# Group weights loaded from ScalarE's queue, rows first on SyncE's, and the router's masks turned between two output blocks

## What is computed

```python
x = x + tanh(g_xattn[0]) * xattn0(layernorm(x), ctx, Wq, w_kc_q, w_kc_kv, W_qr, W_kr, Wo)
x = x + tanh(g_ffn[0])   * moe0(layernorm(x), Wr, br, W1, b1, W2, b2, A1, B1, A2, B2)
x = x + tanh(g_xattn[1]) * xattn1(layernorm(x), ctx, Wq, Wkv_expand, Wout)
x = x + tanh(g_ffn[1])   * ffn1(layernorm(x), U, V, W1, b1, W2, b2)

# xattn0: 16 heads, latent attention with rotated keys
q_big = einsum('bshk,hkq->bshq', (h @ Wq.T), w_kc_q);  q_r = einsum('bshq,hqr->bhsr', q_big, W_qr)
kv = kv_c * cos + rotate_half(kv_c) * sin;             k_r = einsum('bld,hdr->bhlr', kv, W_kr)
ctx_c = einsum('bhsl,bld->bhsd', softmax(q_r k_r), kv)
out = einsum('bhsd,hkd->bshk', ctx_c, w_kc_kv).reshape(b, s, H * K) @ Wo.T
# moe0: top 2 of 8 experts; each adds a rank-16 update (A1, B1) to a shared hidden layer of 2048
```

## Time and profile before

| what | us |
|---|---|
| median of three runs | 1389.22 (1384.52 to 1389.39) |
| the profiled execution, its own time | 1386.96 |
| its span in the trace | 1385.0 |
| TensorE busy in the span | 1354.4 (98%) |
| VectorE busy | 920.6 (66%) |
| ScalarE busy | 517.3 (37%) |
| GpSimd busy | 418.3 (30%) |
| DMA queue of SyncE, share of 16 engines | 29.2% |

### The profile page before, as it was taken

How to read it: one execution, slowest core, us unless ns; L and a number is a source line. 1 busy time by engine, 2 the same in 40 slices (tenths; PEclk the granted TensorE clock), 3 DMA queues, 4 the chain that set the end, 5 groups by cost and what they waited for, 6 DMA issues and landing times.

```text
span 1385.0 us, 20435 instructions
## 1 busy us (share of the span) xinstructions
PE 1354.4 (98%) x7644; PEld 1097.6 (79%) x7644; DVE 920.6 (66%) x1775; ACT 517.3 (37%) x1569; POOL 418.3 (30%) x463
## 2 busy tenths in 40 slices
PE   7899999999999999999999999999999999999999
PEld 5688888888788788878887888788876788878887
DVE  5566566665674777786678667776988777734443
ACT  2444454444464322231113111311137777712221
POOL 3122423222254443201111112114428865530000
PEclk9899999999999999999999999999999999999999
DMA  7643444333454232210121112112334131131111
GB/s 265 183 143 112 145 145 129 123 113 124 134 156 119 80 94 73 82 56 17 45 88 31 50 39 84 43 46 74 101 110 134 43 104 64 60 118 50 54 46 46
DMA packets 98246, 128.90 MB, mean 93 GB/s; under 512 B 11724, under 2 KB 58956, under 8 KB 98148
## 3 DMA queue, kind: packets, MB, share of 16 engines
q1 hardware_dynamic: 98148, 127.60, 29.2%
HBM read 90.86 MB, written 36.70 MB: 92 GB/s over the span
## 4 chain that ended last, share of the span: by engine, by line
PE 85%; DVE 7%; DMA 3%; ACT 2%; issue 1%; SPq 1%; POOL 1%; DVEq 0%; ACTq 0%
PE bank L118 81%; PE bank L121 4%; DMA PYZ<-pscr 2%; SPq L170 1%; DMA pscr<-PYZ 1%; DVE PYZ L164 1%; ACT Pb L124 1%; DVE XR L140 1%; DVE XR L137 1%; DVE AH L130 0%; DVE STG L130 0%; ACT PT L124 0%; DVE st L152 0%; DMA XR<-in_x_dram 0%; DVE sm L146 0%
## 5 line engine op out<-in xcount | busy, mean ns | idle before, releaser
L118 PE MATMUL bank<-XT,AR 128*128 128x512 f32 x1152 | 280.3, 393 | 0.3 <-DVE AR L130 0.2
L118 PE MATMUL bank<-AR 128*128 128x512 f32 x1056 | 262.3, 397 | 6.0 <-DVE Msb L127 5.0
L118 PEld LDWEIGHTS bank<-XT,AR 128*128 128x128 f32 x1152 | 213.8, 188 | 48.6 <-issue 1.5
L118 PEld LDWEIGHTS bank<-AR 128*128 128x128 f32 x1056 | 193.7, 188 | 52.4 <-DVE Msb L127 5.4
L124 ACT ACTIVATE STG<-bank,b1c 128x512 f32<-128x512 f32 x128 | 88.3, 690 | 388.9 <-PE bank L118 321.1
L118 PE MATMUL bank<-AR,CT 128*128 128x512 f32 x768 | 194.3, 397 | 1.7 <-DVE CT L130 1.7
L118 PE MATMUL bank<-AR,AH 128*128 128x512 f32 x768 | 185.9, 390 | 0.0
L118 PEld LDWEIGHTS bank<-AR,AH 128*128 128x128 f32 x768 | 143.6, 188 | 30.7 <-issue 1.1
L127 DVE CAST AH<-STG 128x512 fp32r<-128x512 f32 x192 | 92.7, 483 | 112.1 <-PE bank L118 96.9
L118 PEld LDWEIGHTS bank<-AR,CT 128*128 128x128 f32 x768 | 141.2, 190 | 30.4 <-DVE CT L130 2.6
L127 POOL CAST BA<-STG 128x256 fp32r<-128x256 f32 x64 | 31.0, 485 | 400.0 <-PE bank L118 251.8
(11 more groups left out here) (138 smaller groups left out, 1872.0 us busy)
## 6 DMA issues: line engine op xcount, KB each, us to landing
pscr<-PYZ SPq DMA_DIRECT2D x30, 512.0 KB, 2.9
PYZ<-pscr SPq DMA_DIRECT2D x120, 128.0 KB, 3.0
XR<-scr SPq DMA_DIRECT2D x52, 256.0 KB, 2.8
XR<-in_x_dram SPq DMA_DIRECT2D x32, 256.0 KB, 4.1
scr<-XR SPq DMA_DIRECT2D x32, 256.0 KB, 2.2
STG<-in_Wq_dram SPq DMA_DIRECT2D x8, 512.0 KB, 5.3
STG<-in_WoT_dram SPq DMA_DIRECT2D x8, 512.0 KB, 6.6
STG<-in_W1L_dram SPq DMA_DIRECT2D x16, 256.0 KB, 2.7
```

The lines of the kernel that those rows point to most:

```text
L118: return self.e.matmul(o, w, x, start=start, stop=stop, skip_group_check=True) if self.e else Nothing()
```

## The change

- The weight loads of the groups leave SyncE. A new `prep_load(p)` issues all five from ScalarE: groups 0 and 1 at the start of its program, each later group right after ScalarE's evictions of the group whose buffer it takes (`prep_b(old)`).
- On SyncE x tile 0 comes first, then ident, x tiles 1 to 3, ctx, cs, WkrT, and then g4 and the two bf16 constants, which have a semaphore of their own (`d_ib`); their readers, in the third phase, now wait for it.
- In round 33 the transposes of the masks stand between `wo1(31, (0,))` and `wo1(31, (1,))`.
- On VectorE, `final1` of blocks 2 and 3 stands behind the CT remainders and the row turn (u = 11, 19, 27), and at the end behind `masks_b`. In `router_b` the three instructions on w12c and w1c stand behind the mask values; `tail_x` waits for them.

```diff
+        d_ib = sig("d_ib", 16)
...
-            pe.wait_ge(*d_id[2])
             prep_a(0)
+            pe.wait_ge(*d_id[0])
...
-                    wo1(31, (0, 1))
+                    wo1(31, (0,))
+                    mask_turn(0, 7)
+                    wo1(31, (1,))
...
+            def prep_load(p):
+                g, old = stg_of(p), stg_before.get(p)
+                if old is not None:
+                    ac.wait_ge(*ps.full(("M", old)))
+                    ac.wait_ge(*ps.full(("G", old, 1)))
+                    ac.wait_ge(*ps.full(("A", old)))
+                ac.dma(sKq[g], i["kcqT"][p]).then_inc(*d_Kq[g].mark(p))
+                ac.dma(sWr[g], i["Wqr"][p]).then_inc(*d_Wr[g].mark(p))
+                ac.dma(sKc[g], i["kckv"][p]).then_inc(*d_Kc[g].mark(p))
+                ac.dma(sWo[g], i["WoT"][p]).then_inc(*d_Wo[g].mark(p))
+                ac.dma(sWq[g], i["Wq0"][p]).then_inc(*d_Wq[g].mark(p))
+
             def prep_b(p):
                 for h in range(2):
                     ac.wait_ge(*ps.full(("G", p, h)))
                     hi_of(("G", p, h), GG[p][h][0], ps.ap(("G", p, h))[:, :])
                 ac.wait_ge(*ps.full(("A", p)))
                 hi_of(("A", p), GA[p][0], ps.ap(("A", p))[:, :])
+                for n, old in stg_before.items():
+                    if old == p:
+                        prep_load(n)
...
+            prep_load(0)
+            prep_load(1)
             ac.wait_ge(*d_g[0])
             ac.act(tg[:, :], g4[:, :], ACT.Tanh).then_inc(*c_tg.mark(0))
...
-                if 4 <= u < NU and (u - 4) % 8 == 7:
-                    final1((u - 4) // 8, 2)
-                    final1((u - 4) // 8, 3)
-                if u == 34:
-                    final1(3, 2)
-                    final1(3, 3)
...
                 if u < NU and 3 <= p <= 6:
                     ln_turn(*after1(m), p - 3)
+                if 4 <= u < NU and (u - 4) % 8 == 7:
+                    final1((u - 4) // 8, 2)
+                    final1((u - 4) // 8, 3)
...
                     masks_b(0)
+                    final1(3, 2)
+                    final1(3, 3)
```

More of the change, by code:

```diff
@@ L850, in tensor @@
                     stA0(0)
-                    wo1(31, (0, 1))
+                    wo1(31, (0,))
+                    mask_turn(0, 7)
+                    wo1(31, (1,))
                 if u == 34:
                     wo1(31, (2, 3))
-                if u == 33:
-                    mask_turn(0, 7)
                 if u == 32:
@@ L946, in scores3 @@
                 ks = [ps.take(("s3", u, j), 4 + j) for j in range(4)]
+                pe.wait_ge(*d_ib[1])
                 for j in range(4):
@@ L1384, in seed3 @@
             def seed3(u, j):
+                ac.wait_ge(*d_ib[1])
                 ac.wait_ge(*ex_ok["3", u - 1, j])
@@ L1622, in router_a @@
                     e.max_index(ix[:, tb, :], m8[:, tb, :], rt[:, tb, :]).then_inc(*ix_ok.mark((m, tb)))
+            w1_at = {}
             def router_b(m):
@@ L1628, in router_b @@
                 r1 = chain(e.recip(S(2), m8[:, :, 0]))
-                q2 = chain(e.tt(w12c[:, par, :], m8[:, :, 0], m8[:, :, 1], ALU.add))
                 iob = io8[:, :].unsqueeze(1).to_broadcast([128, 4, 8])
@@ L1639, in router_b @@
                 e2 = chain(e.ts(mB, mB, 2.0, None, ALU.mult, None))
-                e.wait_ge(*q2)
-                chain(e.ts(w12c[:, par, :], w12c[:, par, :], tg[:, 1:2], None, ALU.mult, None))
-                chain(e.ts(w1c[:, par, :], m8[:, :, 0], tg[:, 1:2], None, ALU.mult, None))
                 e.wait_ge(*r)
@@ L1647, in router_b @@
                 e.tt(mB, mB, mA, ALU.subtract).then_inc(*ms_ok.mark(m))
+                q2 = chain(e.tt(w12c[:, par, :], m8[:, :, 0], m8[:, :, 1], ALU.add))
+                e.wait_ge(*q2)
+                chain(e.ts(w12c[:, par, :], w12c[:, par, :], tg[:, 1:2], None, ALU.mult, None))
+                w1_at[m] = chain(e.ts(w1c[:, par, :], m8[:, :, 0], tg[:, 1:2], None, ALU.mult, None))
             def mask_turn(m):
@@ L1762, in tail_x @@
             def tail_x(m, tbs):
+                e.wait_ge(*w1_at[m])
                 for tb in tbs:
@@ L1849, in seed3 @@
             def seed3(u, j):
+                e.wait_ge(*d_ib[1])
                 e.wait_ge(*ex_ok["3", u - 1, j])
@@ L2190, in x_store @@
                 e.dma(rows(ph + 1, m, tb), xr_ap(*key)).then_inc(*t_xr[xr_at[key]].mark(key))
[L2192 to L2207, removed]
             def p_store(u):
@@ L2263, in ba_load @@
                 e.dma(sBA[:, 128:256], i["A2T"][128 * f:128 * f + 128, :]).then_inc(*d_ba.mark((F, 1)))
+            ln_load(0, 0, 0)
             e.dma(ident[:, :], i["ident"]).then_inc(*d_id.mark(0))
[L2266 to L2270, removed]
             for tb in range(1, 4):
                 ln_load(0, 0, tb)
+            kv_load(0)
             e.dma(cs[:, :, :], i["cs"]).then_inc(*d_cs.mark(0))
-            kv_load(0)
-            prep_b(0)
             e.dma(Pb[:, 0:1024], i["WkrT"]).then_inc(*d_wk.mark(0))
-            prep_a(1)
-            prep_b(1)
+            e.dma(g4[:, :], i["g4"]).then_inc(*d_g.mark(0))
+            e.dma(idb[:, :], i["identb"]).then_inc(*d_ib.mark(0))
+            e.dma(mkb[:, :], i["maskb"]).then_inc(*d_ib.mark(1))
             for u in range(NU + 3):
                 m, p = divmod(u, 8)
[L2281 to L2284, removed]
                 if u < NU and 2 <= p <= 4:
@@ L2289, in sync @@
                     p_load(u - 2)
-                if u == 5:
-                    prep_b(7)
                 if u >= 32:
```

## The result

| what | before | after |
|---|---|---|
| median of 20 runs each, alternating on one chip, us | 1386.21 (1383.80 to 1390.07) | 1393.37 (1388.33 to 1398.75) |
| ratio, with its 95% interval | | 1.0049 (1.0038 to 1.0060) |
| the profiled execution, its own time, us | 1386.96 | 1394.02 |
| its span, us | 1385.0 | 1392.2 |

The change costs 7.2 us, in the median and between the two traces alike. The forecast was 1383.2 with a range to 1391: wrong in sign and outside the range.

The account below looks back on a forecast made before the run. TensorE is busy 1354.4 of 1385.0 us, so only its idle and lower-clock time can be won. From 1386.96, +4.3 - 3.2 - 1.2 + 0.8 - 1.5 - 3.0 = -3.8 gives 1383.2 us, range 1375.5 to 1391.

Parts of the forecast that it names:

- P's round trip: Store and reload of P: reload issued and landing earlier, TensorE's stall shrinks from 5.0 to 1.8 us, 3.2 us won.
- Rival 3: Reload of P not earlier, since the weight group ahead fills the engines as before; 1387.6 us, chance 0.10.
- The start: Before TensorE has work: cs and g4 land late as queues share by rows, kv ready 4.3 us later.
- Rival 1: At the start the queues share by bytes: 0.6 us gained instead of 4.3 lost; 1378.3 us, chance 0.30.
- The clock behind the long wait: After the stall on P's round trip: a shorter stretch at half rate, 1.2 us won, bounds 0 and 2.7.
- Group 7: Its weights wait for ScalarE's eviction of A of group 6: a new TensorE wait of 0.8 us near 106.
- Final blocks: VectorE's final blocks moved behind CT and the row turn: TensorE's three waits for CT go, 1.5 us won.
- Masks: Router's masks near 460 us: mask values ready earlier, shorter waits and no fall of the clock, 3.0 us won.
- Rival 2: Issues on ScalarE are dear, at 1.04 us TensorE waits in each round: 17 us, 1400 us, chance 0.06.
- The sign after 480 us: Stages after 480 us: nothing expected; any wait growing there would show the forecast wrong.

Follow-up runs that it names:

- late5: Kernel `rounds` with group 5's issues moved behind ScalarE's split of P of round 0; 1387.08 us against 1386.57 for the kernel before, ratio 1.0005.
- rounds: Kernel before with only groups 2 to 7 issued from ScalarE, opening unchanged; 1393.63 us against 1387.65, ratio 1.0046.
- moves: Kernel before with only the VectorE and TensorE moves (masks, final blocks, w12c and w1c), loads unchanged; 1383.78 us against 1387.65, ratio 0.9975.
- g4early: The changed kernel with g4 issued right behind ident; 1395.61 us against 1387.65 for the kernel before, ratio 1.0072.
- rows1k: Kernel `rounds` with kcqT, WoT and Wq in rows of 1 KB, same bytes; 1390.33 us against 1386.57 for the kernel before, ratio 1.0020.
- opening1k: Kernel `opening` with kcqT, WoT and Wq in rows of 1 KB, same bytes; 1388.39 us against 1386.31 for the kernel before, ratio 1.0011.
- opening: Kernel before with groups 0 and 1 issued from ScalarE and SyncE's new order, later groups on SyncE; 1393.16 us against 1387.65, ratio 1.0049.

## Why the prediction was wrong, point by point

**P's round trip: forecast -3.2, measured +3.2. This is the step that failed.** At k of group 3 after is 9.4 us behind, where the start had left it 6.2. The step put the store between 2.9 and "some 5 us", and the reload at 49 to 51.5 with the engines to itself. Both were wrong. The store took 7.1 us beside group 4, and did not move in the first 3.7 of them. The sum of bytes would have shown it: from ScalarE's first issue, at 45.28, 1,728 KB of weights, the 512 KB store and the 256 KB row load share the engines. At the 366 KB per us of the prediction these are 6.8 us, and with the 2.4 us that its own formula has besides the bytes (3.1 - 0.7) the last of them lands at 54.5; the store landed at 54.94. And the reload was not alone: group 5's issues start with the eviction at 54.80, 0.15 us before it. I had those five issues in the sum as work of ScalarE ahead of the split, but not as traffic beside the reload. The same sum, 1,728 and 512 KB from 54.95, puts its end at 63.5; it was 64.17. `late5` shows that this is what costs. The start had been costed by turns of rows; here, with the same two queues, I priced a mild sharing. Bounds "0 to 4.5" excluded a loss without a reason. And the 5.0 us from which the term was taken was one execution at the dear end; against the usual 3.6 to 4.2 the error of this step is larger still, as `rounds` shows with +6.0 us.

**Rival 3** ("the reload is not earlier", 0.10, 1387.6) was the nearest, but it too ended at no gain. No case had the reload later than before, which is what happened.

**The start: forecast +4.3, measured +6.2.** The rule chosen was right: cs was forecast for 16.6 and landed at 16.0, g4 for 18.0 and landed at 18.0. Rival 1, sharing by bytes, falls with it (g4 at 13.9; its working adds the 4.4 us to 11.3 where cs was put at 11.1, which changes nothing). The kv transposes are 3.4 us late, not 4.3. The term was too small by the clock, which adds 2.8 us behind them: the four G matmuls took 3.62 us instead of 1.88, the transposes and A the rest. The text named this and left it to the range, "to +6"; with 4 us of idle time against the 5.01 that had brought the clock to 0.50 in the earlier trace rows it belonged in the sum.

**The clock behind the long wait: forecast -1.2, measured about -1.6**, from +9.4 to +7.85. The wait is longer, not shorter, so the reason given is wrong and the size is right by chance: the clock is back before 74 us, so more of the slow stretch lies in the wait itself, where it costs nothing:

```profile
64.00:66.00 2.00, 0.00 (x0) 0.00 (x0) 0.72 (x1) 1.06 (x1) 0.00 (x0) 0.50 0.00 0
...
72.00:74.00 2.00, 2.00 (x5) 1.07 (x5) 1.45 (x3) 1.06 (x3) 1.06 (x2) 0.57 0.86 247
```

**Group 7: forecast +0.8, measured 0.** The term let the first issue begin when the eviction ended. It begins with it, 110.39 and 110.40, so the data come 0.6 us earlier, and the second transfer took 3.2 us and not 3.5: it landed at 113.97, 0.2 us before its use, where the wait was 0.8 by estimate. The eviction that follows is held back, as said, and nobody waits for it.

**Final blocks: forecast -1.5, measured -0.95** (-1.3 in `moves`)**.** The three waits for CT are gone. The exponentials, named as what is left, keep more of it than I allowed.

**Masks: forecast -3.0, measured -2.8.** The hold moved from w1c to other instructions, as the low bound feared: w12c took 1.24 us at 468.05, beside a GpSimd instruction of 1.33 at 467.94. But it now stands behind the mask values. The clock stays at 1.00.

**Rival 2, dear issues on ScalarE (0.06):** they took 0.34 to 0.46 us in the main part, so the mechanism is refuted. (Its price was also for seven groups; groups 2 to 7 are six, so 15 us and not 17.) The result went to its side for another reason. That is the second lesson on the chances: I had only one mechanism for "slower", and gave contention, which I had found in the start, no case in the rounds.

**The sign after 480 us.** No wait was to grow there. One did: TensorE waits 0.7 us for a context load at 1031 us, where before has 0.2. It is small, and nothing here says whether the change did it.

**One thing the forecast could not have had.** Between rounds 29 and 30 after loses 2.97 us: its reload of P landed 1.4 us later than in before, the wait on the exponentials is 1.96 us, and the clock falls for some 3 us. No load of this stage was changed. Over all kernels here this stretch takes 12.1 to 15.8 us, 12.9 in before, 15.7 in `rounds`, 13.6 in `g4early`, which has the whole change but for g4's place, and 13.5 in `moves`. I take it for scatter of the single executions; that the change raises its odds was not tested. Without it, the trace would be 4 us behind and not 7, while the 20 runs say 7.2. The dear round trip in before's own trace would fill that gap: with the 2.3 to 2.6 us that the three other kernels gain on it, the parts come to 6.4 to 6.7 us without round 30. That is an estimate from single executions, and which of the two it is stays open.

Summed as the traces show it: +6.2 + 3.2 - 1.6 + 0 - 0.95 + 2.97 - 2.8 = +7.0, with 0.2 over the last 900 us.

## What to carry to other kernels

A second issuing engine does not only save issue time: it sets its transfers against those of the first, and here it was the first queue that lost, in the start by the shortness of its rows. Before moving bulk loads to another queue, list what is on the critical path in the first queue during those microseconds, charge it the bulk's bytes as if they passed first, and do this at every place where the two meet, not only at the first. Here that sum gives 16.6, 54.5 and 63.5 us for cs, the store and the reload, which landed at 16.0, 54.9 and 64.2. Where one queue is enough, the order inside it is the cheaper tool: the reload put ahead of three loads gave 3.0 us, and the whole version with one queue 9.1, of which 3.9 are the moves on VectorE and TensorE.

## What the runs showed of the hardware that was not expected

A store that is queued beside another queue's loads can stand still for microseconds, and in that time the loads are slow as well. In `late5` the store of P is issued at 41.62, 2.5 us after group 4. The windows show busy engines at half the rate, and then the full one:

```profile
42.00:44.00 2.00, 2.00 (x10) 1.65 (x9) 1.30 (x4) 1.40 (x9) 0.00 (x0) 1.00 0.92 184
...
46.00:48.00 2.00, 2.00 (x15) 1.53 (x14) 1.50 (x3) 1.19 (x2) 0.84 (x1) 1.00 1.01 395
```

The slow stretch is not the one in which both move. From 42 to 45.5 us all packets are of ScalarE's queue, and SyncE's come from 45.8 on, at the full rate (the two stretches by queue: packets, MB, share of 16 engines):

```profile
q10 hardware_dynamic: 312, 0.70, 93.5%
...
q1 hardware_dynamic: 287, 0.79, 43.6%
q10 hardware_dynamic: 145, 0.50, 30.7%
```

The first packet of the store comes 3.7 to 4.2 us after its issue in after, `rounds`, `g4early` and `late5`, 2.7 us in `rows1k`, and 0.8 us in before. Why was not tried; it is part of why `rounds` lost so much.

ScalarE starts a DMA issue while the eviction ahead of it in its program still runs (0.60 us at 110.39, the issue at 110.40). And in `opening1k`, whose weights have 1 KB rows, one of ScalarE's issues took 3.5 us (at 7.26), where the same issue in `opening` took 0.46.
